# Masked queries of even and odd heads: written by ScalarE from PSUM, in place of VectorE copies

## The reference, cut to what matters

```
qkv = x @ w_qkv.T + b_qkv                      # q, k, v: 16 heads of 16 columns
inter  = (qb * decay_q) @ S                    # S: the state of the chunks before, 16 x 16 a head
scores = (qb @ kb.T) * dmask                   # within the chunk, causal with decay
intra  = scores @ vb
S      = lam_c * S + (kb * decay_k).T @ vb
out    = (inter + intra) @ w_out.T + b_out
```

## Time and profile before

| what | us |
|---|---|
| three runs, median (lowest to highest) | 900.64 (897.62 to 901.39) |
| the profiled execution's own time | 900.55 |
| its span, first to last instruction | 898.7 |
| PE busy | 699.3 (78%) |
| DVE busy | 545.9 (61%) |
| ACT busy | 304.1 (34%) |
| POOL busy | 452.8 (50%) |
| mean granted clock of TensorE, share of full | 0.868 |

### The profile page before, as it was taken

The page is one execution under the profiler, slowest core; times in us unless marked ns, Lnnn a source line. Parts: engine busy times, 40 slices in busy tenths (PEclk is TensorE's granted clock), DMA queues, the critical chain, the costliest instruction groups (busy, mean ns, idle before and its releaser), DMA issues.

```text
span 898.7 us, 20863 instructions
## 1 busy us (share of the span) xinstructions
PE 699.3 (78%) x6526; PEld 611.6 (68%) x6527; DVE 545.9 (61%) x1067; ACT 304.1 (34%) x656; POOL 452.8 (50%) x313
## 2 busy tenths in 40 slices
PE   1330069999999999368999997139999999999835
PEld 1220059998888888266777785128999999899734
DVE  6899864455554555137888878964545555455513
ACT  3758733333333333002232222113333333433200
POOL 0054018888888886401000000166888888888520
PEclk9655579999999999757999997559999999999965
DMA  9995004555555555441000002022444444444363
GB/s 308 378 361 186 12 24 77 99 114 91 110 99 105 106 92 100 93 135 43 2 0 0 0 1 94 0 94 54 69 78 71 75 76 76 76 73 74 53 172 132
DMA packets 76736, 85.49 MB, mean 95 GB/s; under 512 B 6944, under 2 KB 68384, under 8 KB 76320
## 3 DMA queue, kind: packets, MB, share of 16 engines
q0 software_dynamic: 26880, 36.72, 24.8%
q1 hardware_dynamic: 49824, 48.37, 16.3%
HBM read 50.98 MB, written 34.08 MB: 95 GB/s over the span
## 4 chain that ended last, share of the span: by engine, by line
PE 71%; DVE 8%; issue 3%; DMA 3%; ACT 1%; POOL 0%; DVEq 0%; SPq 0%; ACTq 0%; POOLq 0%
PE PS L729 66%; PE PS L791 3%; DMA A<-expert_sums 1%; DMA expert_sums<-A,place 1%; DVE A L1212 1%; DVE A L1209 1%; DVE A L1380 1%; DVE A L1122 1%; ACT A L697 1%; DVE X L1335 1%; PE PS L871 0%; DVE A L1272 0%; DVE A L1270 0%; PE PS L891 0%; POOL expert_sums L511 0%
## 5 line engine op out<-in xcount | busy, mean ns | idle before, releaser
L729 PE MATMUL PS<-W,A 128*128 (+1 forms) x2228 | 277.6, 281 | 14.6 <-DVE A L1380 7.4
L729 PE MATMUL PS<-A,W 128*128 128x256 f16 (+1 forms) x2356 | 278.6, 277 | 0.8 <-ACT A L617 0.5
L511 POOL DMA_INDIRECT expert_sums<-A,place x140 | 226.5, 1618 | 72.8 <-issue 39.0
L729 PEld LDWEIGHTS PS<-W,A 128*128 128x128 f16 (+1 forms) x2228 | 227.6, 104 | 46.1 <-DVE A L1380 8.3
L729 PEld LDWEIGHTS PS<-A,W 128*128 (+1 forms) x2356 | 237.7, 110 | 29.1 <-issue 1.2
L496 POOL DMA_INDIRECT A<-xn_rows,token x140 | 178.0, 1272 | 93.2 <-issue 40.8
L697 ACT ACTIVATE A<-PS,b1s 128x256 f32<-128x256 f32 x350 | 135.5, 478 | 198.8 <-PE PS L729 198.8
L1270 DVE CAST A<-A 128x1280 f16<-128x1280 f32 x70 | 58.3, 833 | 229.9 <-ACT A L697 229.9
L1272 DVE TENSOR_TENSOR A<-A 128x1280 f16<-128x1280 f32 x70 | 104.5, 1493 | 2.4
L729 PE MATMUL PS<-A 32*128 32x128 f32 (+3 forms) x1248 | 73.6, 292 | 37.1 <-POOL A L534 35.7
L729 PEld LDWEIGHTS PS<-A 32*128 32x128 f32 (+3 forms) x1248 | 56.8, 153 | 51.4 <-issue 43.0
(11 more groups left out here) (158 smaller groups left out, 443.5 us busy)
## 6 DMA issues: line engine op xcount, KB each, us to landing
W<-w SPq DMA_DIRECT2D x24, 640.0 KB, 11.0
A<-expert_sums SPq DMA_DIRECT2D x16, 512.0 KB, 7.6
expert_sums<-zeros SPq DMA_DIRECT2D x2, 2304.0 KB, 18.9
expert_sums<-zeros SPq DMA_DIRECT2D x12, 384.0 KB
xn_rows<-A SPq DMA_DIRECT2D x8, 512.0 KB, 7.2
A<-b SPq DMA_DIRECT2D x2, 1536.0 KB, 9.9
A<-xn_rows,token POOLq DMA_INDIRECT x140
expert_sums<-A,place POOLq DMA_INDIRECT x140, 3.8
```

The lines of the kernel that those rows point to most:

```text
L511: nc.gpsimd.indirect_dma_start(sums_dram[f][q][:, :], bass.IndirectOffsetOnAxis(ap=place[:, at:at + 1], axis=0), YO[q][:, u * D:(u + 1) * ...
L729: return nc.tensor.matmul(out_, l, r, start=start, stop=stop_, skip_group_check=True)
```

## The change

ACT writes QE and QO itself, straight from PSUM bank 4, as Identity activations with a masked bias (`bqm`) and a per-partition scale (the mask of 0 and 1). They take the place of DVE's L1356 and L1357. ACT has eight activations a tile in place of four, in the order QE0, QO0, KT0, QE1, QO1, KT1, QR0, QR1. DVE's `queries(t)` is left with one instruction, QD, and waits for all eight. Two small DVE instructions at the head of the stage make the masked bias, and ACT waits for them once. The waits on `a_qk` are renumbered, and `a_q` is gone.

```diff
+        bqm = sb("bqm", [P, 2 * G])
...
-        a_q = sem("a_q")
+        a_bias = sem("a_bias")
...   ACT, queries_keys(t)
-                    for n, dst in ((0, QR[:, 0]), (2, KT[:, 0]), (1, QR[:, 1]), (3, KT[:, 1])):
-                        nc.scalar.activation(dst, bank[4][:, n * P:(n + 1) * P], ACT.Identity,
-                                             bias=bqk_s[:, n:n + 1]).then_inc(a_qk, 1)
+                    for g in range(G):
+                        q = bank[4][:, g * P:(g + 1) * P]
+                        for dst, of, mask in ((QE, 0, "even"), (QO, G, "odd")):
+                            nc.scalar.activation(dst[:, g], q, ACT.Identity, bias=bqm[:, of + g:of + g + 1],
+                                                 scale=const(mask)).then_inc(a_qk, 1)
+                        nc.scalar.activation(KT[:, g], bank[4][:, (G + g) * P:(G + g + 1) * P], ACT.Identity,
+                                             bias=bqk_s[:, G + g:G + g + 1]).then_inc(a_qk, 1)
+                    for g in range(G):
+                        nc.scalar.activation(QR[:, g], bank[4][:, g * P:(g + 1) * P], ACT.Identity,
+                                             bias=bqk_s[:, g:g + 1]).then_inc(a_qk, 1)
...   ACT, ahead of queries_keys(0)
+                act.wait_ge(a_bias, 1)
...   PE: columns, values_keys, scores
-                    pe.wait_ge(a_qk, t * 4 + 1)
+                    pe.wait_ge(a_qk, t * 8 + 1)
-                    pe.wait_ge(a_qk, t * 4 + 5)
+                    pe.wait_ge(a_qk, t * 8 + 7)
-                    pe.wait_ge(a_qk, t * 4 + (2 * g + 3))
-                    pe.wait_ge(a_q, t * 2 + (g + 1))
+                    pe.wait_ge(a_qk, t * 8 + (3 * g + 4))
...   DVE, head of attention(), and queries(t)
+                dve.wait_ge(attn_w_in, 16 * 9)
+                v.tensor_scalar(bqm[:, 0:G], bqk_s[:, 0:G], const("even"), None, ALU.mult)
+                v.tensor_scalar(bqm[:, G:2 * G], bqk_s[:, 0:G], const("odd"), None, ALU.mult).then_inc(a_bias, 1)
...
-                    for g in range(G):
-                        dve.wait_ge(a_qk, t * 4 + (2 * g + 2))
-                        v.tensor_scalar(QE[:, g], QR[:, g], const("even"), None, ALU.mult)
-                        v.tensor_scalar(QO[:, g], QR[:, g], const("odd"), None, ALU.mult).then_inc(a_q, 1)
+                    dve.wait_ge(a_qk, t * 8 + 9)
                     v.tensor_tensor(QD, QR, const("decay_q").rearrange("p (g c) -> p g c", g=G),
                                     ALU.mult).then_inc(a_qd, 1)
```

## The result

The changed kernel takes 928.8 us in the median of four runs (926.47 to 929.59), against 900.22 (897.62 to 901.39): a ratio of 1.0317, 95% interval 1.0287 to 1.0347, so 28.6 us or 3.2% slower. The forecast was 921.7 with a range to 927.0: the direction was right, the size 7 us short and out of the range. The profiled execution took 926.47 us, with a span of 924.7.

What follows compares the result with a forecast made beforehand. The prediction took PE to bound the stage, its gap ended by DVE's state update: 15 x 1.38 = 20.7 us plus 0.3 at the head, 21.0 on 900.55, gave 921.7 us (median 0.09 higher); range 914 to 927.

Steps and rivals of the forecast that it cites:

- What bounds the stage, and what the wait does: PE bounds the stage; DVE's wait for eight activations, ahead of the state update, goes straight into PE's gap, 15 times.
- The burst's length: ACT's eight activations ahead of QD: QD 2.70 us after the first start against 1.32, 1.38 later, 20.7 us in all.
- the page's figure: Trainium skill's 93 ns per pointer operand on ACT: pitches 0.386 and 0.293, QD 1.5 us later, about 924 us.
- The other edits: Waits of scores, rows_out and columns in the loop, and the two small bqm instructions: nothing; columns ahead of the loop: +0.3.
- The 0.3 at the head: Ahead of the loop, columns waits for all eight activations, unhidden: 414.22 against PE's 413.96, so +0.3 us.
- The clock: Rival: PE's gap growing to 1.9 us lowers its clock for a quarter of the stage, 25 us more, 947 us; chance 0.04.
- The other side: Rival: DVE's relief starts L1358 to L1380 earlier and closes PE's gap, 6.3 us saved, 894 us; chance 0.04.

Runs made afterwards that it cites:

- e1: Changed kernel with copies QR0 and QR1 moved ahead of group 1's masked copies, so DVE waits for five of the eight activations: 903.9 us.
- e7: Changed kernel with state(t) put ahead of queries(t+1) on DVE, so the wait for eight activations no longer precedes the state update: 905.0 us.
- e5: Kernel before the change with six DVE instructions writing to a spare tile put ahead of QD, delaying it by 0.82 us: 910.6 us.
- e6: Kernel before the change with five longer DVE instructions writing to a spare tile put ahead of QD, making PE's gap 1.78 us: 924.6 us.
- e3: Changed kernel with the masked copies' per-partition scale replaced by the constant 1.0, one pointer operand fewer (mask left out): 915.2 us.
- e2: Changed kernel with three matmuls of no use put into PE's gap ahead of out_proj: 920.3 us.
- e8: Changed kernel with QD behind state(t) and masked(t+1, 0) on DVE, and QR0, QR1 and deviation_ahead behind rows_out(t) on ACT: 894.6 us.
- e4: Kernel before the change with group 1's masked copies QE1 and QO1 made behind the state update on DVE: 891.5 us.

## Why the prediction was wrong, and where it was right

*What bounds the stage, and what the wait does.* Right. A DVE wait for the eighth activation stands ahead of the state update and goes into PE's gap in full, 15 times. e1 and e7 show it by moving the wait, e5 and e6 by putting a delay in its place.

*The burst's length.* Right in kind, 0.12 too long: 1.26 us later, not 1.38. L627 lasts 0.460 us, not 0.475, and two of them take 0.81, so one starts 0.35 after the other, not 0.380; L656's row, with a different source and width, gave 0.03 too much for each start. By e3 the second operand costs 0.09, which is what the Trainium skill states (ScalarE: Activation LUTs, section "What ACT_TABLE_LOAD costs": about 93 ns a pointer operand); the page's figure was the better one for this term, though its pitches of 0.29 and 0.39 were each 0.03 to 0.04 longer than the measured ones, so that its 1.5 us for QD was farther off than the forecast's 1.38. The term came to 18.9 us against 20.7.

*The other edits.* Right: nothing for `scores`, for `columns` in the loop and for the two small instructions; `rows_out` hidden (it ends at 452.30, PE starts at 453.44). The 0.3 at the head is right in part by luck: `columns(1)` starts 412.47 - 409.88 = 2.59 after ACT's first copy against 413.96 - 411.55 = 2.41, so its wait is worth 0.18, and the rest of the 0.33 goes with the clock, which rose later there.

*The clock.* This is the step that failed. The forecast set PE's gap of 1.9 us against the granted clock only as a rival, with a chance of 0.04, on the argument that PE still works four fifths of each period. The changed kernel shows both at once: PE works 7.96 of 9.73 us, the gap is 1.76, and the clock falls in every third period. Its price, too, was guessed as a quarter of the stage, 25 us; it was 5 x 1.68 = 8.4. e2 took it away by filling the gap, e3 by shortening the gap to 1.40, e6 brought it back without the change. With the price as a term and not as a rival the sum would have been 21.0 + 8.4 = 29.4, or 18.9 + 0.3 + 8.4 with the burst as measured: 27.6, which is what the stage shows. The medians lie 28.6 apart; the last 1.0 is within what single executions differ by. The rows before held no such gap at the upper level, so they could give neither the price nor the length that is enough; but the argument that four fifths of work keep the clock up had no row behind it either, and by it the term stood at nothing in the sum.

The Trainium skill had warned of it in kind (TensorE: Matmul & The Clock Gate, section "HAM oscillation — how this bites in real kernels"): a wait that recurs in each tile can throttle TensorE again and again. The waits of its example are of 3 to 5 us, and there the clock falls in each tile. The trace agrees that falls recur with the gaps, but here gaps of 1.76 us are enough, and the clock falls in every third tile.

*The other side.* It did not come: the condition that the forecast set for it, the burst's end within 1.29 us, was not met (2.53). Its place, PE's gap of 0.5 us, was real, and e8 and e4 both close it. But e4 does so with all four masked copies still on DVE, so what the runs show to be worth something is a short way to the state update, not a DVE with less work.

## What to carry to other kernels

Moving work from a busy engine to an idle one helps only if the consumer's wait does not move to the end of a longer burst: look at what is queued behind the wait, and order the burst, and the waiting engine's instructions, so that only what the critical step needs stands ahead of it. A recurring TensorE gap has a second price, the clock: the same 1.26 us of delay cost 18.9 us by itself and 8.4 more through the clock, so a gap longer than any that the trace shows at the upper level should have its price in the sum. And before moving work, try the order on the engine that has it: two instructions put behind the state update (e4) gave at least as much as the change with both of its repairs (e8).

## What the runs showed of the hardware

In the loop the granted clock stayed at 1.00 with a recurring gap of 0.50, 0.76, 0.81, 1.32 and 1.40 us. It fell again and again at 1.76 (every third period, five times) and at 1.78 (after three, four and three periods, four times), in two kernels that make the gap in different ways. A fall lasted some 3 us at 1.2 GHz and cost 1.68 us. Each of these is read from one profiled execution, and nothing was run between 1.40 and 1.76. The longer period alone does not do it: e2 has a period of 9.74 us, a gap of 0.49 and no fall. But in the other kernels a longer gap is also a larger idle share of the period, and the runs do not tell the two apart. ACT's activation of 128 columns from PSUM lasted 0.369 us with one pointer operand and 0.460 with two, and in a row one started every 0.26 or 0.35 us. DVE's copies of 128 x 128 from SBUF that follow one another without a wait between them started 0.14 us apart (e5), where QE and QO, each 0.28 long, are 0.20 apart.
